# One transformer block on one core: text rows first, table sum by transfers, block 0 picked by products, last keys' products stacked

## What is computed

```
h = concat(patches @ proj_w.T + proj_b + pos_embed, txt)            # (8, 164, 192)
xn = layernorm(layernorm(h)) * ln_w
Q[h] = xn * W_qk[h];  P[h] = softmax(causal(Q[h] Q[h]^T / sqrt(192)))   # 12 heads
out[h] = P[h] (xn - mean(wte)) / (position + 1)                      # wte: 50257 x 192
h = h + concat_heads(out) @ W_o.T
x = layernorm(h); n = x * rsqrt(mean(x^2) + 1e-6) * ffn_ln_w
expert = argmax(n @ w_router) of 16, a batch's expert keeps its first 64 rows
y = relu(n @ wi[expert]) @ wo[expert] for kept rows, n for dropped ones
h = h + x + max(softmax(router logits)) * y
```

## Time and profile before

| | |
|---|---|
| median of 3 runs | 368.05 us (366.1 to 369.53) |
| profiled execution | 367.87 us |
| its span (first to last instruction) | 366.0 us |
| granted TensorE clock, mean | 0.967 |

### The profile page before, as it was taken

The page is one execution under the profiler, slowest core; times in us unless marked ns, Lnnn a source line. Parts: engine busy times, 40 slices in busy tenths (PEclk is TensorE's granted clock), DMA queues, the critical chain, the costliest instruction groups (busy, mean ns, idle before and its releaser), DMA issues.

```text
span 366.0 us, 6697 instructions
## 1 busy us (share of the span) xinstructions
PE 334.5 (91%) x2336; PEld 306.0 (84%) x2336; DVE 228.0 (62%) x557; ACT 126.2 (34%) x437; POOL 167.7 (46%) x180
## 2 busy tenths in 40 slices
PE   8499969899999999999998979999949999999992
PEld 3388859799899898997997969999815999999991
DVE  0669768789688787796888977657485222222221
ACT  2056543552545436534545024446610111111110
POOL 3173943755854846657548011250661134444321
PEclk9969989999999999999999978999998999999997
DMA  8899999289999995799997969400232699999940
GB/s 252 264 430 282 260 247 217 77 170 230 219 232 230 196 239 143 139 236 270 246 211 199 324 191 289 112 2 1 100 107 73 183 293 266 266 264 260 266 118 17
DMA packets 21096, 74.29 MB, mean 203 GB/s; under 512 B 3540, under 2 KB 9173, under 8 KB 20306
## 3 DMA queue, kind: packets, MB, share of 16 engines
q1 hardware_dynamic: 11362, 43.16, 38.5%
q0 software_dynamic: 6800, 27.82, 37.0%
q10 hardware_dynamic: 2912, 3.04, 3.0%
HBM read 66.12 MB, written 9.25 MB: 206 GB/s over the span
## 4 chain that ended last, share of the span: by engine, by line
PE 66%; DVE 13%; DMA 8%; ACT 5%; issue 5%; ACTq 1%; POOL 0%; POOLq 0%; DVEq 0%
PE bO L1224 18%; PE bS L1224 15%; PE bE L1224 14%; PE bJ L1224 12%; DMA wx<-in_wte 6%; ACT PB L563 2%; DMA hB<-in_txtB 2%; PE bT L1311 2%; DVE wx L856 1%; PE bT L1576 1%; DVE wbuf L856 1%; PE bT L1317 1%; PE bT L1270 1%; DVE oTA L823 1%; ACT pay L620 1%
## 5 line engine op out<-in xcount | busy, mean ns | idle before, releaser
L423 POOL TENSOR_TENSOR PA<-PA,rn 128x512 f32<-128x512 f32 x24 | 25.4, 1057 | 81.5 <-DVE rn L813 81.5
L401 POOL TENSOR_TENSOR AwA<-zT,w 96x512 f32<-96x512 f32 x45 | 50.1, 1192 | 17.4 <-ACT zT L540 17.4
L1224 PE MATMUL bJ<-wo_sb,oTA 128*128 128x192 f32 x288 | 52.7, 333 | 0.0
L558 ACT ACTIVATE PA<-bS,negmax 128x128 f32<-128x128 f32 x96 | 34.0, 367 | 51.3 <-DVE negmax L801 51.2
L1224 PEld LDWEIGHTS bS<-zT,AwA 96*128 96x128 f32 x384 | 47.3, 194 | 1.3 <-issue 0.2
L1224 PEld LDWEIGHTS bJ<-wo_sb,oTA 128*128 128x128 f32 x288 | 47.4, 194 | 0.0
L1224 PE MATMUL bS<-zT,AwA 96*128 96x128 f32 x384 | 47.1, 276 | 0.0
L1224 PE MATMUL bO<-PA,wx 96*128 96x112 f32 x384 | 45.4, 275 | 0.5 <-DVE PA L1197 0.5
L1224 PEld LDWEIGHTS bO<-PA,wx 96*128 96x128 f32 x384 | 44.9, 192 | 0.7 <-DVE PA L1197 0.7
L468 POOL DMA_INDIRECT out<-PA,yrow x16 | 15.1, 942 | 56.0 <-DVE PA L1213 56.0
L695 ACT ACTIVATE AwA<-bO 128x448 f32<-128x448 f32 x16 | 8.7, 544 | 78.5 <-PE bO L1224 52.9
(11 more groups left out here) (252 smaller groups left out, 705.5 us busy)
## 6 DMA issues: line engine op xcount, KB each, us to landing
wbuf<-in_wte POOLq DMA_DIRECT2D x10, 1344.0 KB, 12.7
wx<-in_wte POOLq DMA_DIRECT2D x8, 1344.0 KB, 12.0
wx<-in_wi SPq DMA_DIRECT2D x16, 576.0 KB
wx<-in_wo SPq DMA_DIRECT2D x16, 576.0 KB
wx<-in_wte SPq DMA_DIRECT2D x12, 672.0 KB, 9.2
dispatched<-zeros SPq DMA_DIRECT2D x7, 675.5 KB, 9.0
wbuf<-in_wte SPq DMA_DIRECT2D x2, 1344.0 KB, 7.0
wx<-in_wte SPq DMA_DIRECT2D x2, 1344.0 KB, 17.6
```

What stands on the lines that cost most here:

```text
L401: nc.gpsimd.tensor_tensor(o, zT[:, k, ss].unsqueeze(1).to_broadcast(list(o.shape)), w2[:, k, hs].unsqueeze(2).to_broadcast(list(o.shape)), ...
L423: nc.gpsimd.tensor_tensor(t, t, q.unsqueeze(2).to_broadcast(list(t.shape)), ALU.mult).then_inc(p_ready, 1)
L558: last = nc.scalar.activation(PA[:, h, :], bank[:, j * SA:(j + 1) * SA], ACT.Exp, bias=negmax[:, h:h + 1], accum_out=lsum[:, h:h + 1])
L1224: return nc.tensor.matmul(o, l, r, start=start, stop=stop, skip_group_check=True)
```

## The change

1. *Text rows first.* Text rows of batches 0 and 1 are loaded first and have semaphores of their own; the rest follows (`txt2_in`, `hb2_in`), and SP's table loads wait for that. `hB` has 108 partitions: the 36 rows three times. Constants come after the small weights. On VectorE the key weights and the statistics of two batches come first, those of six batches before `row_max(0, 0)`; ScalarE copies the second embedding four heads later; one warming product less.
2. *Table slots added by transfers.* `slot_add` goes. POOL issues three accumulating transfers from slot to slot, two ahead of the work for batch 7, one in it. The zeros wait for them. In batch 0, one `plain_sum` moves two steps down.
3. *Block 0 picked by products.* VectorE compares each row's place with 0..111 (`select`), TensorE multiplies the normalised rows of all slots with it into the transposed block 0. The transpose of the scattered rows starts with block 1, whose rows are read first. Making the dropped rows is spread over the first block.
4. *Last keys stacked.* PTB1 and vB have three blocks of 36 keys, (H, H, L) and (H, L, H) by partition ranges, so one product over 108 partitions takes the place of three over 36. POOL writes the three copies of the normalised weights (`last_keys`) into new columns of PB; transposes are 108 x 108.

```
 (SP)
-            for p0, p1 in ((IMG, 116), (116, 128)):
-                sp.dma_start(H[p0:p1, 0:NBATCH, :], txtA[p0 - IMG:p1 - IMG]).then_inc(txt_in, 16)
+            for b0, b1, arrived in ((0, 2, txt_in), (2, NBATCH, txt2_in)):
+                for p0, p1 in ((IMG, 116), (116, 128)):
+                    sp.dma_start(H[p0:p1, b0:b1, :], txtA[p0 - IMG:p1 - IMG, b0:b1]).then_inc(arrived, 16)
...
-            sp.wait_ge(hb_in, 16)
+            sp.wait_ge(hb2_in, 48)
...
-            sp.wait_ge(txt_in, 32)
+            sp.wait_ge(txt2_in, 32)
...
+            sp.wait_ge(fold_in, 16 * 3)
             sp.wait_ge(zero_ready, 1)
...
-            for q in range(XBUF - 1):
+            for q in (1, 0, 2):
                 rows(sp, q, q)
 (POOL)
+            def fold(s, t, before):
+
+                for w in (s, t):
+                    pool.wait_ge(wte_in[w], slot_loads(w))
+                if before:
+                    pool.wait_ge(fold_in, 16 * before)
+                pool.dma_start(wchunk[s], wchunk[t], accum_op=ALU.add,
+                               max_dma_last_dim=WR * EMB * 4 // 2).then_inc(fold_in, 16)
...
+            def last_keys():
+
+                for q0 in (0, 2):
+                    t, k = PB[:, q0:q0 + 2, SEQ:SEQ + SR].rearrange("p q (t s) -> p q t s", t=3), PB[:, q0:q0 + 2, SA:SEQ]
+                    nc.gpsimd.tensor_tensor(t, k.unsqueeze(2).to_broadcast(list(t.shape)),
+                                            rn[0:HB * SB, 12 + q0:14 + q0].unsqueeze(2).unsqueeze(3).to_broadcast(list(t.shape)),
+                                            ALU.mult).then_inc(pb_ready, 1)
...
+                if folds:
+                    fold(2, 3, 0)
+                    fold(0, 1, 0)
                 weigh(b + 1, n, (0, 1), (0,))
                 normalise(b, range(3, SPR))
                 weigh(b + 1, n, (0, 1), (1,))
                 for c in chunks[0:1]:
                     add_wte(c)
+                last_keys()
                 weigh(b + 1, n, (0, 1), (2,))
+                if folds:
+                    fold(0, 2, 2)
                 normalise(b + 1, (0,))
 (ACT)
+            for t in range(3):
+                act.dma_start(hB[t * SB:(t + 1) * SB, 0:2, :], txtB[:, 0:2]).then_inc(hb_in, 16)
...
+            act.dma_start(cst[:], cst_d).then_inc(cst_in, 16)
+            for t in range(3):
+                act.dma_start(hB[t * SB:(t + 1) * SB, 2:NBATCH, :], txtB[:, 2:NBATCH]).then_inc(hb2_in, 16)
 (DVE)
-                plain_sum(b, 1)
+                else:
+                    plain_sum(b, 1)
                 t_low(b, 3)
                 row_factor(b + 1, 0)
                 t_low(b, 4)
                 row_max(b + 1, 1)
+                if is0(b):
+                    plain_sum(b, 1)
                 plain_sum(b, 2)
...
-            slot_add(2, 3)
-            slot_add(0, 1)
-            slot_add(0, 2)
+            plain_total()
+            table_total()
             residual_b(0)
-            table_total()
...
             base_factors(1)
+            select(0)
             residual_b(2)
...
             place(1)
+            select(1)
 (DVE, block 0: after the relu, then the copy of block 1; the index after block 0's sum)
+                if start:
+                    dropped_rows()
                 xt_copy(b + 1)
...
+                if start:
+                    dropped_index()
 (PE)
-                        mm(oo, vA[x][:, 0:E0], PTB0[y][:, :, :], i == 0, False)
-                        last = mm(oo, vB[x][:, 0:E0], PTB1[y][:, :, :], False, i == 2)
+                        last = mm(oo, vA[x][:, 0:E0], PTB0[y][:, :, :], i == 0, False)
+                if g == 3:
+                    last = mm(oo, vB[:, 0:E0], PTB1[:, :, :], False, True)
...
-            stay_warm(bJ, 3)
+            pe.wait_ge(sel_ready, 2)
+            pe.wait_ge(cen_ready, STAGE[0][1])
+            dispatch(0, 3)
...
             expert_rank(1)
-            stay_warm(bJ, 10)
+            dispatch(3, STAGE[0][1])
+            stay_warm(bJ, 8)
+            pe.wait_ge(sel_ready, 3)
+            pe.wait_ge(cen_ready, SLOTS)
+            dispatch(STAGE[0][1], SLOTS).then_inc(xT_sum, 1)
             pe.wait_ge(be_ready, 1)
...
-            stay_warm(bJ, 26)
-            x_transpose(0, 16)
...
                 last.then_inc(y_sum, 1)
+                if start:
+                    stay_warm(bJ, 6)
+                    x_transpose(1, 16)
```

More of the change, by code:

```diff
@@ L699, in block_step @@
                 hidden(b)
-                if not (is0(i) and q == 0):
+                if is0(i) and q == 0:
+                    act.wait_ge(scattered, 16 * SLOTS)
+                else:
                     act.wait_ge(y_ready, b)
@@ L1174, in _, with xt_copy, dropped_norms, dropped_rows @@
             nc.vector.tensor_reduce(beC[:, :], bex[:, :], X, ALU.add).then_inc(be_ready, 1)
+            def xt_copy(b):
+                dve.wait_ge(xT_sum, b + 1)
+                nc.vector.tensor_tensor(xT, bT[1][0:EC, 0:2 * T].rearrange("p (k n) -> p k n", k=2),
+                                        flc[:, :].unsqueeze(2).to_broadcast([EC, 2, T]), ALU.mult).then_inc(xT_ready, 1)
+            def dropped_norms():
+                dve.wait_ge(base_ready, SLOTS)
+                for j0, j1 in ((0, 6), (6, 8), (8, 10), (10, 11)):
+                    n, b0 = j1 - j0, ORD[j0]
+                    last = nc.vector.tensor_tensor(drow[:, b0:b0 + n, :], norm[:, j0:j1, :],
+                                                   flnb[:, :].unsqueeze(1).to_broadcast([128, n, EMB]), ALU.mult)
+                link(last)
+            def dropped_rows():
+                for j in range(SLOTS):
+                    n = 128 if ORD[j] < NBATCH else BP
+                    nc.vector.scalar_tensor_tensor(drow[0:n, ORD[j], :], drow[0:n, ORD[j], :], pay[0:n, j, D_RP:D_RP + 1], base[0:n, j, :], ALU.mult, ALU.add)
+            def dropped_index():
+                link(nc.vector.tensor_reduce(kept[:, :], kp[:, :, :], X, ALU.add))
+                link(nc.vector.scalar_tensor_tensor(dropF[:, :], kept[:, :], float(BIG), pay[:, :, D_ROW], ALU.mult, ALU.add))
+                nc.vector.tensor_copy(dropI[:, :], dropF[:, :]).then_inc(drop_ready, 1)
+            xt_copy(0)
             dve.wait_ge(be_row, 1)
@@ L1344, in value @@
                     for i, (x, y) in enumerate(SPLIT):
-                        first, final = odd == 0 and i == 0, odd == 1 and i == 2
+                        first, final = odd == 0 and i == 0, g < 3 and odd == 1 and i == 2
                         if g < 3:
@@ L1351, in value @@
                             mm(ee, vA[x][:, part], PTB0[y][:, odd:HEADS:2, :], first, False)
[L1352 removed]
+                    if g == 3:
+                        last = mm(ee, vB[:, part], PTB1[:, odd:HEADS:2, :], False, odd == 1)
                 last.then_inc(e_ready, 1)
@@ L1560, in _, with dispatch @@
             logits(10, 11, 7)
-            stay_warm(bJ, 3)
+            def dispatch(k0, k1):
+                for j in range(k0, k1):
+                    j0, _, sel = sels[j >= 6]
+                    for k in range(2):
+                        last = mm(bT[1][0:EC, k * T:(k + 1) * T], norm[:, j, k * EC:(k + 1) * EC], sel[:, j - j0, :],
+                                  j == 0 and k == 0, j == SLOTS - 1)
+                return last
+            pe.wait_ge(sel_ready, 2)
+            pe.wait_ge(cen_ready, STAGE[0][1])
+            dispatch(0, 3)
             pe.wait_ge(oh_ready, 2)
@@ L1591, in block_step @@
                 last.then_inc(h1_sum, 1)
-                x_transpose((q + 1) % XBUF, (i + 1 + (q + 1) // XBUF) * 16)
+                start = is0(i) and q == 0
+                if not start:
+                    x_transpose((q + 1) % XBUF, (i + 1 + (q + 1) // XBUF) * 16)
                 pe.wait_ge(wox_in[q], turn)
                 pe.wait_ge(h0_ready, b + 1)
-                if not (is0(i) and q == 0):
+                if not start:
                     pe.wait_ge(y_ready, b)
```

166 lines of the change are left out of this document (88 added, 78 removed).

## The result

The changed kernel takes 382.67 us (median of 4 runs, 382.29 to 384.42), the kernel before 367.6 us beside it; the ratio is 1.0419, with a 95% interval of 1.0367 to 1.047. I had forecast 376.6 us with a range up to 381. So the direction was right and the size was not: +15.1 us by the medians, where the sum said +8.6. The profiled execution of the changed kernel took 384.42 us, a span of 382.5 and 1.92 around it, against 366.0 and 1.87.

A forecast was written before the change was run, and what follows sets the result against it. From 55 us on almost only TensorE was taken to bound the kernel, with VectorE level in the batches. 367.87 + 4.9 (start) - 3.0 (last keys) + 9.6 (table) - 2.8 (block 0) = 376.6 us; range 362 to 381.

The forecast's parts named there:

- Start: Start of the kernel: embedding begins earlier, but plain table rows land later, so value products start at 56.7, +4.9 us.
- I take 1.5: Start: estimated delay in us of SP's first table load, from loading the last 36 text rows three times.
- the term for the turns: Start: SP's waiting packets each cost 0.4 us beside POOL's accumulating loads; 15.5 packets, 6.2 us.
- my 54: Start: time in us taken for the plain table rows to land.
- my own 55.5: Start: landing time of the plain table rows by the sum 47.8 + 1.5 + 6.2.
- Last keys: Batches: stacked products save TensorE 0.83 us a batch, of which 0.4 counts in batches 0 to 5, 0.6 in 6; -3.0 us.
- The bound by VectorE: Batches: VectorE is level with TensorE, so TensorE's 0.83 us pay only as far as VectorE comes earlier, up to 0.6.
- Table: Table sum: three accumulating transfers replace VectorE's adds; the sum is there at 224.4 in place of 214.8, +9.6 us.
- The chain with its three links: Table: three transfers, 6.4 us each, one behind another after the last load, landing at 201.8, 208.2 and 219.8.
- the rival of the fast folds: Table: transfers inside SBUF run at the plain rate, 3.2 us each; sum 3.1 us late, 370.1 us; chance 0.18.
- Block 0: Block loop: block 0 starts seven us earlier, runs 6.5 us on a cold clock, dropped rows follow; -2.8 us.
- The transfers keep pace: Start: rival "Faster", plain rows land 20.5 us after issue, at 41; with fast folds too, 359.7 us; chance 0.14.

The follow-up runs named there:

- a_lateacc: The changed kernel with POOL's first two accumulating loads (chunks 4 and 5) issued only just ahead of chunk 6: 363.45 us.
- a_small: The changed kernel with the small loads cst2 and wtail issued behind the first plain table rows: 375.48 us.
- quarter_packets: The changed kernel with POOL's accumulating loads in packets of half the size, same bytes and order: 372.18 us.
- before_sp_late: The kernel before with SP's table loads waiting in addition for VectorE's first token add: 374.28 us.
- one_copy: The changed kernel with the last 36 keys' products apart again and hB loaded in one copy, not three: 383.61 us.
- before_late: The kernel before with only POOL's chunks 4 and 5 issued just ahead of chunk 6: 363.89 us.
- late_nofold_unstack: late_nofold with the last 36 keys' products apart again, hB's three copies kept: 355.09 us.
- late_nofold: The changed kernel with VectorE adding the slots again (no folds) and POOL's chunks 4 and 5 issued just ahead of chunk 6: 352.3 us.
- late_warm: late_nofold with seven warming products where TensorE waits for the count of blocks: 350.45 us.
- late_one_fold: late_nofold with one fold: slots 2 and 3 are added by a transfer, the other two additions stay on VectorE: 350.76 us.

## Why the forecast was wrong, step by step

The profiled execution took 384.42 us, 7.8 more than the 376.6 of the forecast. By the marks 4.2 of them are the start, 0.1 the last keys, 1.8 the table and 1.7 block 0.

**Start, the term that failed: +4.9 said, +9.1 measured.** The mechanism on record (two queues take turns, each waiting packet of SP's costs a turn of POOL's) is shown by four runs (a_lateacc, a_small, quarter_packets, before_sp_late). What was mis-sized is "I take 1.5" for SP's delay: it was 3.55. For the extra copies I had 1.0 us by their bytes and 0.5 for small packets; they cost 2.0 (15.99 against one_copy's 13.97; ScalarE's queue moved 0.36 MB in 2 us with 104 packets, from 12 to 14 us). The new order I had put at nothing; SP now waits for the last of more and smaller text loads, and that is the other 1.5 (13.97 against 12.44). The 4.7 us by which POOL's loads come sooner were 2.7, since POOL waits for SP's first chunks (1.78 and 2.83 us in the timeline), which I overlooked. By luck the two errors left the relative shift at 6.2 us, so the term for the turns came out nearly right, and the late start came on top. Of the 4.6 us between my 54 and the measured 58.64, 2.05 are this delay; 1.5 is that I then chose 54 below my own 55.5, for the third accumulate that might not be there (it was, at 40.72, and the two queues were full until 58 us); and about 1 lies in the turns, for which I had 6.2 us and the estimate of 2.15 gives 7.2. The rest of the working held: 2.9 us from the plain rows to the value products, where I had 2.7. With the accumulates late in both kernels the start is worth what its front promised: from 60.49 in before_late to 54.94 in late_nofold_unstack it is 5.6 us.

**Last keys, -3.0 said.** Measured 3.17 at the payload, but spread otherwise: 0.69 us a batch and not 0.4, of which 0.9 were given back between batch 5 and the mean. That the sum fits is in part luck. The bound by VectorE was weaker in the loop than I had read from the earlier trace rows. Its cost in the load I put into the start.

**Table, +9.6 said, 10.4 measured.** The chain with its three links was right. Counted from the last load's issue at 190.48, which is 6.2 us behind that of the earlier trace rows, I had the third landing at 226.0; it landed at about 227.3. A fold, from SBUF to SBUF, is not faster than an accumulate from HBM: q0 moves 0.43 MB in 2 us here as well, from 198 to 200 us:

```profile
q0 software_dynamic: 80, 0.43, 105.5%
```

The rule of the Trainium skill that I weighed (DMA: Bandwidth & Descriptors, Anatomy of one DMA, and Bandwidth) would have given 5.2 us a fold; the folds took 14.4, 12.9 and 9.8 us from issue to landing, the last of them alone in its queue. The measurement decides against it, and the rival of the fast folds fell with it.

**Block 0, -2.8 said, -1.1 in the changed kernel.** The working fits late_nofold, where the clock came back in time: block 0 took the 6.5 us that I had said, and the gain was 2.74. Here the cold clock lasted through all of block 0 (8.15 us): a mean of 0.57 over eight microseconds, where late_nofold had 0.79. Why it recovers sooner in one kernel than in the other, whose instructions there are the same and whose gap ahead is as long (1.79 us against 1.80), stays open; that it need not fall at all is shown by late_warm.

**Rivals.** "The transfers keep pace", on record with 359.7 us, did not happen, but it is what a_lateacc makes true: 363.45 us with all four parts in place. Sum of the terms as measured: 367.87 + 9.1 - 2.9 + 10.4 - 1.1 gives 383.4, and the profiled execution had 384.42; the missing microsecond lies between batch 5 and the mean, where the table above has 11.4 for the folds' 10.4.

## What to carry to other kernels

When two queues had work at once, the engines gave each a packet in turn: a transfer that somebody waits for should neither have small packets ahead of it in its queue nor big accumulating ones beside it. Price such an edit by the stretch in which the urgent queue is alone; here each us lost of it cost an estimated 2.15, as long as nothing moved the later accumulates. An addition given to a transfer was a gain where it waited for nothing late, and cost its whole landing time where it stood behind the last load. Where a moved piece of work starts sooner behind an idle gap, try to fill the gap with products: behind 1.8 us without them block 0 ran at half the clock for all or part of its time.

## What the runs showed that I had not expected

VectorE's sum of 576 elements, both operands in SBUF, took 8.74 us in the changed kernel and 8.68 in a_small. The two lines are of the changed kernel and of late_one_fold:

```profile
205.24 8.74 DVE L899 TENSOR_TENSOR wx<-wx 128x576 f32<-128x576 f32 x1
```

```profile
194.35 0.76 DVE L903 TENSOR_TENSOR wx<-wx 128x576 f32<-128x576 f32 x1
```

In late_one_fold POOL has nothing to do then. In the changed kernel POOL runs an unbroken series of products from 204.76 to 213.4, and the sum ends 0.6 us behind it. It cost nothing here, inside the wait for the folds. The Trainium skill, SBUF — State Buffer, Who interferes with whom, has such an operation contend with POOL's reads; the numbers agree, though I had not thought that it would stand through a whole series. And halving the accumulates' packets did not make the queues slower together: they moved 0.70 MB in the 2 us shown above, not 0.64. The accumulates themselves came a little later: POOL's loads into wbuf land after 13.0 us in the median and not 12.8, those into wx after 14.0 and not 12.0.
